# Row maxima of attention scores taken per head, with a signal for each, instead of per step of two heads

## The chip, the cores and the metric

The kernel runs on one core of a Trainium2 chip. The metric is the device time of one execution in microseconds (us). The engines are PE (TensorE: matmuls and, as PEld, their weight loads), DVE (VectorE), ACT (ScalarE), POOL (GpSimd) and SP (SyncE, which here only issues DMAs). Each engine works through its own list of instructions in order, and semaphores tie the lists together.

## The reference

Cross-attention over 64 samples. The input of each sample is normalised over all its 64 x 256 values, 8 heads of 64 channels attend from 256 queries to 256 keys of the context, and the result is projected and added to the input.

```python
# x: (64, 64, 256) = input (n, c, s); ctx_2048: (64, 64, 256) = context; h = 8 heads, c = 64 channels, all float32
mu = jnp.mean(input, axis=(1, 2), keepdims=True)
var = jnp.var(input, axis=(1, 2), keepdims=True)
xn = (input - mu) * jax.lax.rsqrt(var + EPS)
xn = xn * gamma[None, :, None] + beta[None, :, None]
q = jnp.einsum('oc,ncs->nos', Wq, xn) + bq[None, :, None]
kv = jnp.einsum('od,nds->nos', Wkv, context) + bkv[None, :, None]
q = q.reshape(n, h, c, s).transpose(0, 1, 3, 2)
kv = kv.reshape(n, 2 * h, c, -1).transpose(0, 1, 3, 2)
k, v = (kv[:, :h], kv[:, h:])
scale = c ** (-0.25)
att = jax.nn.softmax(jnp.einsum('nhqc,nhkc->nhqk', q * scale, k * scale), axis=-1)
y = jnp.einsum('nhqk,nhkc->nhqc', att, v)
y = y.transpose(0, 1, 3, 2).reshape(n, h * c, s)
out = jnp.einsum('co,nos->ncs', Wo, y) + bo[None, :, None]
return input + out
```

## The kernel before, in words

Two samples form a pair, and there are 32 pairs. A pair has 16 heads, which are worked on in eight steps of two heads each (`STEPS = 8`, `UNITS = 16`). The key and value projections are folded into other matrices at the start, so that the scores of a head are one product of transformed queries `t` with the raw context `c2`, and the attention result is a mix of context rows.

For step k of a pair these operations follow on each other:

1. `scores` (PE, L367): eight matmuls fill two banks of PSUM, `fill[k % 2][:, o, :]`, one bank of 512 columns for each head o (two query tiles of 256 keys). They wait until the exponentials of step k-2 have read both banks, and end with one signal, `scored`.
2. `row_max` (DVE, L538): one reduction reads both banks, 1024 columns, and writes the four negated maxima (2 heads x 2 query tiles). It ends with one signal, `max_ready`.
3. `exponentials` (ACT, L483): four activations of 256 columns, each followed by a read of its accumulator (the row sum). They wait for `max_ready` and signal `exp_ready` once per head.
4. `reciprocal` (DVE, L544): waits for both heads of the step.
5. `divide` (POOL, L639): 1024 columns, in place.
6. `turn` (DVE, L551): transposes the probabilities in blocks of 32, 1024 columns.
7. `mix` (PE, L401): items 0 to 3 belong to the pair's first sample, 4 to 7 to the second. Item 0 waits for transpose 3 (the transpose of step 3), and item 4 for transpose 7. The items 0 and 4 are followed by three more of their sample. After the items 3 and 7 ACT copies `z` (L499), and PE projects the output (L410).

Beside the steps run the normalisation of a pair ahead: statistics (DVE, L567), a matmul with ones for the mean (PE, L422), the small DVE operations of the spread (L577 to L583), a second such matmul (L426), the root (POOL, L649), the two normalisations (POOL, L654), the projection to `t` in `z` (PE, L379) and its copies (ACT, L492).

The order of the work on each engine is written out by hand. `PE_ORDER`, `ACT_ORDER`, `DVE_ORDER` and `POOL_ORDER` give each item a time in units of a sixteenth of a pair; each engine sorts its items by that time modulo 16, and an item whose time is 16 or more, or negative, belongs to the pair before, or to one ahead. Within one pair DVE runs, by this: transpose 5 of the pair before, max 0, reciprocal 7, the means, transpose 6, max 1, reciprocal 0, transpose 7 (still of the pair before), max 2, reciprocal 1, transpose 0, max 3, reciprocal 2, transpose 1, max 4, reciprocal 3, transpose 2, max 5, the spread, transpose 3, the result, reciprocal 4, the variance, max 6, the transpose of the context, reciprocal 5, max 7, transpose 4, the statistics, reciprocal 6. PE runs: scores 0 and 1, projection, scores 2, mixes 4 and 5 of the pair before, scores 3, mix 6, scores 4, mix 7, scores 5, the mean, the output projection, the spread's matmul, scores 6 and 7, mixes 0 to 3. ACT runs: copy of z, exponentials 0, the four copies to `t`, exponentials 1 to 3, copy of z, exponentials 4 to 7. POOL runs: divisions 0 to 3, division 4, root, division 5, the normalisations, divisions 6 and 7. A number behind an operation's name is always its step.

The DMAs are issued from SP, in an order of their own, and the change touches none of them.

Of the kernel before, what the change touches and what calls it, by code (L numbers as in the profile page):

```python
# [6 lines left out]
ALU = mybir.AluOpType  # L7
ACT = mybir.ActivationFunctionType
AX = mybir.AxisListType
# [12 lines left out]
UNITS = PS * H  # L22
STEPS = UNITS // 2
QT = S // 128
# [6 lines left out]
PAIRS_OF_BANKS = 2  # L31
# [60 lines left out]
def work(pair, order):  # L92
    for at, kind, item in in_order(order):
        owner = pair.shift(-int(at // UNITS))
        if owner.exists():
            yield kind, item, owner


def wait(eng, sem, value):
    if not isinstance(value, int) or value > 0:  # L100
        eng.wait_ge(sem, value)  # L101
# [6 lines left out]
def walk(eng, steps):  # L108
    for c in range(-3, 3):
        steps(Pair(0, c))  # L110
    with eng.Fori(0, (NPAIR - 8) // 2) as j:
        steps(Pair(j, 3))
        steps(Pair(j, 4))
    for c in range(NPAIR - 5, NPAIR + 2):
        steps(Pair(0, c))


def build(nc, x, ctx, gamma, beta, Wq, bq, Wkv, bkv, Wo, bo, out):
    stack = ExitStack()
    with stack:  # L120
        def sb(name, shape, dt=F32):
            return stack.enter_context(nc.sbuf_tensor(name, shape, dt))

        def pb(name, shape):
            return stack.enter_context(nc.psum_tensor(name, shape, F32))

        def sem(name):
            return stack.enter_context(nc.semaphore(name))
# [44 lines left out]
        t = [sb(f"t_{i}", [128, HP, PS, S]) for i in range(2)]  # L173
        neg_max = sb("neg_max", [128, STEPS, 2 * QT])
# [8 lines left out]
        fill = [pb(f"fill_{i}", [128, 2, 512]) for i in range(PAIRS_OF_BANKS)]  # L183
# [28 lines left out]
        max_ready = sem("max_ready")  # L212
# [19 lines left out]
        def load_weights(eng, weights, loaded):  # L232
            for dst, src in weights:
                eng.dma_start(dst, src, allow_slow_non_contiguous=True).then_inc(loaded, 16)  # L234
# [216 lines left out]
        @block.scalar  # L451
        def _(act):
            def query_key_steps():
                act.wait_ge(qk_loaded, 16 * QK_DMAS)
                act.mul(gamma_scaled[:, :], gamma2[:, :], SCALE).then_inc(w_act, 1)
                act.wait_ge(w_mm, 1)
                for i in range(2):
                    act.copy(qk[:, i::2, :], fill[0][:, i, 0:HP * CK].rearrange("r (p c) -> r p c", p=HP)
                             ).then_inc(w_act, 1)
                act.wait_ge(w_mm, 2)  # L460
                for i in range(2):
                    act.copy(wo_t2[:, :, i, :], fill[1][:, 1, 0:HP * C].rearrange("r (p c) -> r p c", p=HP)
                             ).then_inc(w_act, 1)
                act.wait_ge(w_dve, 3)

            def output_value_steps():
                act.wait_ge(w_mm, 4)
                banks = (fill[1][:, 1, :], fill[0][:, 1, :])
                for i in range(2):
                    r = 64 * i  # L470
                    act.copy(u[r:r + 64, :, :], banks[i][r:r + 64, 0:HP * C].rearrange("r (p c) -> r p c", p=HP)
                             ).then_inc(w_act, 1)

            def exponentials(pair, k):
                wait(act, max_ready, pair.count(STEPS, k + 1))
                owner, before = (pair, k - SLOTS) if k >= SLOTS else (pair.shift(-1), k - SLOTS + STEPS)
                if owner.exists():
                    wait(act, turned, owner.count(STEPS, before + 1))
                for o in range(2):
                    bank = fill[k % PAIRS_OF_BANKS][:, o, :]  # L480
                    for qt in range(QT):
                        g = QT * o + qt
                        ins = act.activation(probs[:, k % SLOTS, g, :], bank[:, K * qt:K * qt + K], ACT.Exp,  # L483
                                             bias=neg_max[:, k, g:g + 1], accum_out=denom[:, k, g:g + 1])
                    ins.then_inc(exp_ready, 1)

            def query_rows(pair, hp):
                if hp % 2 == 0:
                    wait(act, projected, pair.count(HP // 2, hp // 2 + 1))
                if pair.shift(-2).exists():  # L490
                    wait(act, scored, pair.shift(-2).count(STEPS, HP + hp + 1))
                act.activation(t[pair.parity()][:, hp, :, :], z[:, hp, :], ACT.Identity,  # L492
                               bias=d_col[:, hp:hp + 1]).then_inc(t_ready, 1)

            def copy_z(pair, s):
                wait(act, mixed, pair.count(PS, s + 1))
                if s == 0 and pair.shift(-1).exists():
                    wait(act, summed_out, pair.shift(-1).count(1, 1))
                act.copy(z_sb[:, s, :, :].rearrange("p h (t a j) -> p a (h t) j", t=QT, a=QB),  # L499
                         z[:, :, S * s:S * s + S].rearrange("p a (g j) -> p a g j", j=32)).then_inc(z_ready, 1)  # L500

            def steps(pair):
                for kind, item, owner in work(pair, ACT_ORDER):
                    if kind == "t":
                        if owner.first():
                            if item == 0:
                                query_key_steps()
                            elif item == 2:
                                output_value_steps()
                        query_rows(owner, item)  # L510
                    elif kind == "exp":
                        exponentials(owner, item)
                    else:
                        copy_z(owner, item)

            load_weights(act, qk_weights, qk_loaded)
            load_weights(act, out_weights, weights_loaded)
            walk(act, steps)

        @block.vector  # L520
        def _(dve):
# [13 lines left out]

            def row_max(pair, k):
                wait(dve, scored, pair.count(STEPS, k + 1))
                dve.tensor_reduce(neg_max[:, k, :],  # L538
                                  fill[k % PAIRS_OF_BANKS][:, :, :].rearrange("p o (t k) -> p (o t) k", t=QT),
                                  AX.X, ALU.max, negate=True).then_inc(max_ready, 1)  # L540

            def reciprocal(pair, k):
                wait(dve, exp_ready, pair.count(UNITS, 2 * k + 2))
# [53 lines left out]
            def steps(pair):  # L597
                for kind, item, owner in work(pair, DVE_ORDER):
                    if kind == "weights":
                        if owner.first() and item == 0:  # L600
                            query_key_steps()
                        elif owner.first():
                            output_value_steps()
                    elif kind == "max":
                        row_max(owner, item)
                    elif kind == "recip":
                        reciprocal(owner, item)
                    elif kind == "turn":
                        turn(owner, item)
                    elif kind == "moments":  # L610
                        channel_moments(owner)

                        wait(dve, moments_ready, owner.count(PS, PS))
                    elif kind == "mean_var":
                        channel_mean_var(owner)
                    elif kind == "spread":
                        channel_spread(owner)
                    elif kind == "sample_var":
                        sample_variance(owner)
                    elif kind == "turn_context":  # L620
                        turn_context(owner)
                    elif kind == "result":
                        result(owner)
# [66 lines left out]
```

## Time and profile before

| | us |
|---|---|
| median of 3 runs | 808.37 |
| lowest and highest of them | 806.89, 810.76 |
| the profiled execution | 807.66 |
| its span | 805.8 |
| mean granted TensorE clock | 0.983 of full |

The profile is of one execution. Its span goes from the first to the last instruction on the core; the execution's time is 1.86 us longer. The page gives the busy time of each engine and its share of the span. The timeline lists instructions with their start and their duration; a merged row has a count behind it (x8), and its duration reaches from the start of the first to the end of the last. In brackets stands the idle time of the engine ahead of the row and what ended it. On one engine an instruction may start before the recorded end of the one ahead of it.

### The profile page before, as it was taken

The page shows a single profiled execution, that of the slowest core. Times are in us where ns is not written, and L with a number is a line of the kernel's source. Part 1 is how long each engine was busy: PE and PEld are TensorE (multiplying, and loading weights), DVE is VectorE, ACT ScalarE, POOL GpSimd, SP SyncE. Part 2 cuts the span into 40 slices and gives each one's busy share as a digit, 9 for nine tenths or more (in the row PEclk, how much of TensorE's full clock was granted, in tenths as well). Part 3 has the DMA queues.
Part 4 walks back from the last instruction along what each step waited for, and adds up shares of the span by engine and source line. Part 5 has one row for each costly group of instructions (what it writes and reads, how often), then busy time and mean ns, then how long its engine had stood idle before and what let it go on. Part 6 is the DMA issues. An engine that isn't in the chain of part 4 may idle for free.

```text
span 805.8 us, 29956 instructions
## 1 busy us (share of the span) xinstructions
PE 686.3 (85%) x11204; PEld 445.8 (55%) x11204; DVE 678.0 (84%) x1124; ACT 621.6 (77%) x2248; POOL 581.7 (72%) x360
## 2 busy tenths in 40 slices
PE   5689988889888888988888988888898888898886
PEld 4355655555655555655555655555565555566453
DVE  1589888898988889898889898888989888989883
ACT  2578778787788878687878788878778778878872
POOL 1478677777777878677877777788777687777763
PEclk9989999999999999999999999999999999999998
DMA  5112222222221222222222221221222122222110
GB/s 111 37 48 68 62 57 67 60 62 62 62 63 51 72 52 64 59 62 53 68 59 58 62 64 52 64 72 51 62 62 62 49 72 53 64 65 52 44 40 15
DMA packets 74814, 47.56 MB, mean 59 GB/s; under 512 B 33748, under 2 KB 74708, under 8 KB 74772
## 3 DMA queue, kind: packets, MB, share of 16 engines
q1 hardware_dynamic: 72848, 46.59, 21.6%
q10 hardware_dynamic: 1924, 0.40, 0.3%
q8 instruction: 28, 0.46, 0.2%
q14 instruction: 14, 0.11, 0.0%
HBM read 25.96 MB, written 4.19 MB: 37 GB/s over the span
## 4 chain that ended last, share of the span: by engine, by line
POOL 41%; issue 37%; PE 9%; DVE 9%; ACT 2%; POOLq 1%; DMA 1%; SPq 1%; ACTq 0%; DVEq 0%
POOL probs L639 32%; POOL xhat L654 6%; DVE probs_t L551 4%; PE z L401 4%; DVE neg_max L538 3%; PE fill L367 3%; POOL rstd L649 3%; ACT probs L483 2%; POOLq L101 1%; PE z L379 1%; DMA wv<-in_L_xattn_Wkv 1%; ACT t L492 1%; DVE recip L544 0%; DVE y L594 0%; SPq L234 0%
## 5 line engine op out<-in xcount | busy, mean ns | idle before, releaser
L639 POOL TENSOR_TENSOR probs<-probs,recip 128x1024 f32<-128x1024 f32 x256 | 483.1, 1893 | 188.5 <-DVE recip L544 184.3
L483 ACT ACTIVATE probs<-fill,neg_max 128x256 f32<-128x256 f32 x1024 | 470.5, 483 | 149.9 <-DVE neg_max L538 149.6
L551 DVE STREAM_TRANSPOSE probs_t<-probs 128x1024 f32<-128x1024 f32 x256 | 313.7, 1225 | 49.7 <-POOL probs L639 46.2
L538 DVE TENSOR_REDUCE neg_max<-fill 128x4 f32<-128x1024 f32 x256 | 306.6, 1198 | 36.3 <-PE fill L367 36.0
L401 PE MATMUL z<-probs_t,ctx_keys 32*64 32x256 f32 x8192 | 260.3, 388 | 69.5 <-DVE probs_t L551 68.3
L367 PE MATMUL fill<-c,t 64*128 64x256 f32 x2048 | 285.6, 404 | 17.6 <-ACT probs L483 13.2
L401 PEld LDWEIGHTS z<-probs_t,ctx_keys 32*64 32x64 f32 x8192 | 177.0, 134 | 139.5 <-issue 69.7
L367 PEld LDWEIGHTS fill<-c,t 64*128 64x128 f32 x2048 | 182.8, 189 | 120.0 <-ACT probs L483 58.4
L483 ACT ACTIVATION_READ_ACCUMULATOR probs<-fill,neg_max 128x1 f32 x1024 | 220.1, 215 | 0.0
L492 ACT ACTIVATE t<-z,d_col 128x512 f32<-128x512 f32 x128 | 77.8, 708 | 7.3 <-PE z L379 7.3
L379 PE MATMUL z<-xhat,qk_gamma 64*128 64x512 f32 x256 | 66.5, 637 | 16.2 <-POOL xhat L654 16.2
L654 POOL TENSOR_SCALAR xhat<-x,mean,rstd 128x256 f32<-128x256 f32 x64 | 77.6, 1222 | 0.2
L499 ACT COPY z_sb<-z 128x1024 f32<-128x1024 f32 x64 | 65.4, 1021 | 11.5 <-PE z L401 10.5
L410 PE MATMUL z<-z_sb,u 128*64 128x256 f32 x512 | 62.3, 385 | 1.2 <-ACT z_sb L499 1.2
L379 PEld LDWEIGHTS z<-xhat,qk_gamma 64*128 64x128 f32 x256 | 23.1, 193 | 43.3 <-issue 38.3
L544 DVE RECIPROCAL recip<-denom 128x4 f32<-128x4 f32 x256 | 41.0, 160 | 6.3 <-ACT probs L483 2.7
L410 PEld LDWEIGHTS z<-z_sb,u 128*64 128x64 f32 x512 | 33.9, 136 | 16.6 <-ACT z_sb L499 2.3
L649 POOL TENSOR_TENSOR rstd<-variance,minus_half 128x2 f32<-128x2 f32 x32 | 22.8, 712 | 21.1 <-DVE variance L587 21.1
L567 DVE BATCH_NORM_STATS2 moments<-x 128x6 f32<-128x256 f32 x64 | 22.8, 398 | 9.3 <-DMA x<-in_x 9.3
L594 DVE SCALAR_TENSOR_TENSOR y<-z,out_bias,x_res 128x256 f32<-128x256 f32 x32 | 14.2, 445 | 9.6 <-PE z L410 9.6
L422 PEld LDWEIGHTS z<-mean_var,ones 128*128 128x128 f32 x64 | 10.1, 199 | 20.5 <-issue 16.5
L422 PE MATMUL z<-mean_var,ones 128*128 128x2 f32 x64 | 12.6, 267 | 8.1 <-DVE mean_var L571 6.7
(38 smaller groups left out, 91.1 us busy)
## 6 DMA issues: line engine op xcount, KB each, us to landing
ctx_keys<-ctx_turned SPq DMA_DIRECT2D x512, 32.0 KB, 1.8
x<-in_x SPq DMA_DIRECT2D x64, 128.0 KB, 2.8
c<-in_ctx SPq DMA_DIRECT2D x64, 128.0 KB, 2.7
ctx_rows<-in_ctx SPq DMA_DIRECT2D x128, 32.0 KB, 1.8
x_res<-in_x SPq DMA_DIRECT2D x32, 128.0 KB, 2.2
out<-y SPq DMA_DIRECT2D x32, 128.0 KB, 1.8
wq<-in_L_xattn_Wq ACTq DMA_DIRECT2D x2, 128.0 KB
wv<-in_L_xattn_Wkv SPq DMA_DIRECT2D x2, 128.0 KB
```

What stands on the lines that cost most here:

```text
L367: mm = pe.matmul(banks[:, o, K * qt:K * qt + K], t[p][r:r + 64, hp, s, 128 * qt:128 * qt + 128], c2[p][r:r + 64, s, :], start=True, stop=True)
L379: mm = pe.matmul(z[:, hp, :], qk_gamma[r:r + 64, 2 * hp:2 * hp + 2, :], xhat[r:r + 64, :, :], start=True, stop=True)
L401: mm = pe.matmul(z[64 * g:64 * g + 64, a, S * s:S * s + S], ctx_keys[p][r:r + 32, b, s, :], probs_t[p][r:r + 32, s, b, g, :, :, :], start= ...
L410: mm = pe.matmul(z[64 * s:64 * s + 64, 0, 0:S], u[:, hp, :], z_sb[:, s, hp, :], start=(hp == 0), stop=(hp == HP - 1))
L483: ins = act.activation(probs[:, k % SLOTS, g, :], bank[:, K * qt:K * qt + K], ACT.Exp, bias=neg_max[:, k, g:g + 1], accum_out=denom[:, k, ...
L492: act.activation(t[pair.parity()][:, hp, :, :], z[:, hp, :], ACT.Identity, bias=d_col[:, hp:hp + 1]).then_inc(t_ready, 1)
L499: act.copy(z_sb[:, s, :, :].rearrange("p h (t a j) -> p a (h t) j", t=QT, a=QB), z[:, :, S * s:S * s + S].rearrange("p a (g j) -> p a g j" ...
L538: dve.tensor_reduce(neg_max[:, k, :], fill[k % PAIRS_OF_BANKS][:, :, :].rearrange("p o (t k) -> p (o t) k", t=QT), AX.X, ALU.max, negate=T ...
L551: dve.transpose(probs_t[p][:, s, :, :, hp, :, :].rearrange("p b o t j -> p o t b j"), probs[:, k % SLOTS, :, :].rearrange("p (o t) (b j) - ...
L639: pool.tensor_tensor(p, p, recip[:, k, :].unsqueeze(2).broadcast_to([128, 2 * QT, K]), ALU.mult).then_inc(probs_ready, 1)
L649: pool.tensor_tensor(rstd[:, :], variance[:, :], minus_half[:, :], ALU.pow).then_inc(rstd_ready, 1)
L654: pool.tensor_scalar(xhat[:, s, :], x2[p][:, s, :], mean[:, s:s + 1], rstd[:, s:s + 1], ALU.subtract, ALU.mult).then_inc(xhat_ready, 1)
```

## The change

The maximum of a step is taken in two reductions, one for each head: 512 columns of one bank each, the first two and the last two of the step's four maxima. Each of them raises `max_ready`, which so counts heads (`UNITS`, 16 a pair) and no longer steps. ACT no longer waits ahead of the step's four activations for the step's maximum, but ahead of each head's two activations for the maximum of that head. The wait for `turned` (a free slot of `probs`) now stands ahead of the wait for the maximum. Nothing else is changed.

```diff
--- before.py
+++ after.py
@@ -472,11 +472,11 @@
                              ).then_inc(w_act, 1)
 
             def exponentials(pair, k):
-                wait(act, max_ready, pair.count(STEPS, k + 1))
                 owner, before = (pair, k - SLOTS) if k >= SLOTS else (pair.shift(-1), k - SLOTS + STEPS)
                 if owner.exists():
                     wait(act, turned, owner.count(STEPS, before + 1))
                 for o in range(2):
+                    wait(act, max_ready, pair.count(UNITS, 2 * k + o + 1))
                     bank = fill[k % PAIRS_OF_BANKS][:, o, :]
                     for qt in range(QT):
                         g = QT * o + qt
@@ -535,9 +535,10 @@
 
             def row_max(pair, k):
                 wait(dve, scored, pair.count(STEPS, k + 1))
-                dve.tensor_reduce(neg_max[:, k, :],
-                                  fill[k % PAIRS_OF_BANKS][:, :, :].rearrange("p o (t k) -> p (o t) k", t=QT),
-                                  AX.X, ALU.max, negate=True).then_inc(max_ready, 1)
+                for o in range(2):
+                    dve.tensor_reduce(neg_max[:, k, QT * o:QT * o + QT],
+                                      fill[k % PAIRS_OF_BANKS][:, o, :].rearrange("p (t k) -> p t k", t=QT),
+                                      AX.X, ALU.max, negate=True).then_inc(max_ready, 1)
 
             def reciprocal(pair, k):
                 wait(dve, exp_ready, pair.count(UNITS, 2 * k + 2))
```

## Rows read from the trace of the kernel before

**Rows 1.** The page, part 1: busy time of each engine.

```profile
PE 686.3 (85%) x11204; PEld 445.8 (55%) x11204; DVE 678.0 (84%) x1124; ACT 621.6 (77%) x2248; POOL 581.7 (72%) x360
```

**Rows 2.** Timeline of PE: start us, us, engine, line, operation, tiles, count.

```profile
66.11 0.36 PE L422 MATMUL z<-mean_var,ones 128*128 128x2 f32 x2
...
735.87 0.36 PE L422 MATMUL z<-mean_var,ones 128*128 128x2 f32 x2
```

**Rows 3.** Totals of the waits: engine, its line, releaser, us, times, longest.

```profile
ACT probs L483 <- DVE neg_max L538: 149.6, 118, 5.3
```

**Rows 4.** Timeline of DVE, first stretch of the pair; idle time in brackets.

```profile
421.31 1.23 DVE L538 TENSOR_REDUCE neg_max<-fill 128x4 f32<-128x1024 f32 x1 [0.91 <-PE fill L367]
...
426.00 1.19 DVE L538 TENSOR_REDUCE neg_max<-fill 128x4 f32<-128x1024 f32 x1
427.11 0.14 DVE L577 COPY mean<-z 128x2 f32<-128x2 f32 x1
...
429.15 0.17 DVE L544 RECIPROCAL recip<-denom 128x4 f32<-128x4 f32 x1
```

**Rows 5.** Timeline of POOL, the same pair.

```profile
429.39 1.89 POOL L639 TENSOR_TENSOR probs<-probs,recip 128x1024 f32<-128x1024 f32 x1 [2.48 <-DVE recip L544]
...
432.11 1.89 POOL L639 TENSOR_TENSOR probs<-probs,recip 128x1024 f32<-128x1024 f32 x1 [0.16 <-POOL rstd L649]
...
436.38 3.74 POOL L639 TENSOR_TENSOR probs<-probs,recip 128x1024 f32<-128x1024 f32 x2
```

**Rows 6.** Timeline of DVE, second stretch of the pair.

```profile
433.13 0.71 DVE L567 BATCH_NORM_STATS2 moments<-x 128x6 f32<-128x256 f32 x2
...
438.31 1.25 DVE L551 STREAM_TRANSPOSE probs_t<-probs 128x1024 f32<-128x1024 f32 x1 [1.28 <-POOL probs L639]
439.48 1.18 DVE L538 TENSOR_REDUCE neg_max<-fill 128x4 f32<-128x1024 f32 x1
...
440.67 1.21 DVE L551 STREAM_TRANSPOSE probs_t<-probs 128x1024 f32<-128x1024 f32 x1
...
445.10 1.22 DVE L538 TENSOR_REDUCE neg_max<-fill 128x4 f32<-128x1024 f32 x1 [0.73 <-PE fill L367]
```

**Rows 7.** Timeline of PE, the same pair.

```profile
423.31 1.12 PE L401 MATMUL z<-probs_t,ctx_keys 32*64 32x256 f32 x32
...
442.01 1.99 PE L401 MATMUL z<-probs_t,ctx_keys 32*64 32x256 f32 x64 [1.96 <-DVE probs_t L551]
443.92 1.14 PE L367 MATMUL fill<-c,t 64*128 64x256 f32 x8
```

**Rows 8.** Timeline of ACT, the same pair.

```profile
422.57 0.47 ACT L483 ACTIVATE probs<-fill,neg_max 128x256 f32<-128x256 f32 x1 [1.41 <-DVE neg_max L538]
...
424.54 1.01 ACT L499 COPY z_sb<-z 128x1024 f32<-128x1024 f32 x1
```

**Rows 9.** Groups by line and shape: count | busy us, mean ns | idle before.

```profile
L551 DVE STREAM_TRANSPOSE probs_t<-probs 128x1024 f32<-128x1024 f32 x256 | 313.7, 1225 | 49.7 <-POOL probs L639 46.2 <-issue 3.6
L538 DVE TENSOR_REDUCE neg_max<-fill 128x4 f32<-128x1024 f32 x256 | 306.6, 1198 | 36.3 <-PE fill L367 36.0
...
L567 DVE BATCH_NORM_STATS2 moments<-x 128x6 f32<-128x256 f32 x64 | 22.8, 398 | 9.3 <-DMA x<-in_x 9.3
...
L560 DVE STREAM_TRANSPOSE ctx_turned<-ctx_rows 128x256 f32<-128x256 f32 x32 | 13.9, 435 | 0.0
```

**Rows 10.** Timeline of all engines near the start of the run.

```profile
38.14 0.47 ACT L483 ACTIVATE probs<-fill,neg_max 128x256 f32<-128x256 f32 x1 [0.75 <-DVE neg_max L538]
...
40.13 2.08 PE L367 MATMUL fill<-c,t 64*128 64x256 f32 x8 [0.95 <-ACT probs L483]
...
42.25 1.23 DVE L538 TENSOR_REDUCE neg_max<-fill 128x4 f32<-128x1024 f32 x1 [0.60 <-PE fill L367]
```

**Rows 11.** Stretches: start:end, length, busy us (instructions) per engine, PEclk, DMA share, GB/s.

```profile
321.60:325.00 3.40, 3.30 (x66) 2.03 (x66) 2.29 (x3) 2.66 (x12) 2.70 (x2) 0.57 0.25 58
```

**Rows 12.** Timeline of PE, the mixes in that stretch.

```profile
321.70 3.35 PE L401 MATMUL z<-probs_t,ctx_keys 32*64 32x256 f32 x64 [2.42 <-DVE probs_t L551]
```

## The prediction

> **What bounds the kernel now.** I read the page's first part, then the totals of the waits, then the timeline of one steady pair on each engine, because the shares alone decide nothing here: PE is busy for 85%, DVE 84%, ACT 77%, POOL 72% [rows 1]. No engine is full, so the period of a pair (16 heads, eight steps) is set by a cycle that runs through several of them. It is regular: the matmul of the means, once per pair, starts at 66.11 us and 28 pairs on at 735.87, 23.92 us a pair [rows 2]; the pair that I walk takes 445.10 - 421.31 = 23.79 us from its max 3 (the maximum of step 3) to the next.
>
> ACT waits for the maxima for 149.6 us in 118 waits [rows 3], about 4.7 us in each of 32 pairs. That is what the change aims at. The question is whether this idle time lies on the cycle. I followed the cycle from max 3 at 421.31, which starts when its scores land:
> - DVE, with no idle time shown: max 3, reciprocal 2, transpose 1, max 4, reciprocal 3, transpose 2, max 5, the four small operations of the spread, transpose 3, the result, and reciprocal 4 at 429.15 [rows 4]. 7.84 us, three maxima in it.
> - Division 4 starts on POOL at 429.39, 0.24 us on. Behind it POOL runs root, division 5, the two normalisations, divisions 6 and 7, with no gap over 0.16 us [rows 5]. Division 6 ends at 436.38 + 1.89 = 438.27, and DVE's transpose 6, which waited for it, starts at 438.31 [rows 6]: 8.92 us, no maximum in it.
> - DVE: transpose 6, max 1, reciprocal 0, transpose 7, which ends at 440.67 + 1.21 = 441.88 [rows 6]; the mix that waits for it starts on PE at 442.01 [rows 7]. 3.70 us, one maximum.
> - PE: mixes 4 and 5, then scores 3 at 443.92 [rows 7], 1.91 us; and max 3 at 445.10 [rows 6], 1.18 us.
> The sum is 7.84 + 0.24 + 8.92 + 3.70 + 1.91 + 1.18 = 23.79 us, the period. No exponential is in it. Four maxima are: 1, 3, 4 and 5.
>
> **The change part by part.** *Removed:* the first head's exponentials wait no longer for the second head's half of the reduction. Now max 3 starts at 421.31 and the exponentials behind it at 422.57 [rows 4, 8], 1.26 us. How long a half takes: the same kind of operation stands in the trace at two sizes, the transpose with 1225 ns for 1024 columns and 435 ns for 256 [rows 9], so (1225 - 435) / 768 = 1.03 ns a column. 1024 columns are then 1055 ns, and the maximum's 1198 ns [rows 9] holds 143 ns that don't depend on columns. A half takes 527 + 143 = 670 ns, and the first exponentials can start 1198 - 670 = 0.53 us sooner.
>
> What that is worth in a steady pair: behind exponentials 3 ACT copies z at 424.54, and the copy also needs mix 7, which starts at 423.31 and takes 1.12 us, to 424.43 [rows 7, 8]. Of 0.53 us ACT can pass on 0.11 there. Mix 7 stands behind scores 3 in PE's order, so the cycle drives it. Exponentials 0 can start sooner, but the queries' rows behind them on ACT wait for the projection, which waits for POOL's normalisations in the cycle. Reciprocals 4 to 7 come late in DVE's own order and not when their exponentials end. So I value the earlier start at nothing; the POOL and DVE cycle is what covers it. Without that cover the gain is bounded by 0.53 us at one place of a pair.
>
> At the start of the run the cycle isn't closed yet: exponentials 3 wait 0.75 us for their maximum, scores 5 wait 0.95 us for these, and max 5 waits 0.60 us for the scores [rows 10]. The 0.53 us comes through once: -0.5 us. At the end the last z copies stand behind their mixes as above, so nothing there.
>
> *Added on DVE:* a second reduction per step, 256 in all, over the same columns. What it costs, d, decides the forecast. By the nearest rows: max 5 starts at 426.00 and the operation behind it at 427.11 [rows 4], so an overlapped maximum holds DVE for 1.11 us, 55 ns over its columns. The two statistics of 256 columns, like behind like, take 0.71 us together and 398 ns each [rows 6, 9]: the second starts 0.31 us behind the first, 48 ns over its 264 ns. From above: if the second half started only when the record of the first has ended, d would be the whole 143 ns. Zero and less is excluded, since the columns stay and one more instruction has to start. Between the ends I take the value of the rows in which one DVE operation follows another without waiting, 50 ns, and keep 40 to 143.
>
> The Trainium skill (Vector Engine (DVE) Microarchitecture Reference, Measured stream behaviour on trn2) gives built-in operations about 75 ns per instruction after queue overlap, beside the columns. The rows here show 48 and 55. By the page's figure the sum below would be 125 x 0.075 - 0.5 = +8.9 us, an estimate from that page.
>
> Where d counts: in the four maxima of the cycle, 4 x 50 = 0.20 us a pair. What is queued behind the longer maximum is the reciprocal and the transpose of older steps, and POOL's division and PE's mixes behind these; that is the cycle, counted once. Maxima 6, 7 and 0 lie between reciprocal 4 and the 1.28 us for which DVE waits before transpose 6, and max 2 lies ahead of the 0.73 us of wait before max 3 [rows 6]; 3d is 0.15 us, 0.43 at most, so these four are hidden. Without that cover d would count eight times, 0.40 us a pair.
>
> *Added on ACT:* one more wait per step. It is met when it is reached: the second half ends about 0.6 us behind the first, while the first head's two exponentials and their accumulator reads take 0.9 us of the step's 1.8. Its own handling can't be read from a row; between nothing and 0.1 us, 0.8 us a pair, it stays under the 4.7 us that ACT idles, so I take nothing. PE, SP and POOL get no instruction more and no DMA moves. The scores still wait for both heads' exponentials.
>
> *Sum:* 29 pairs x 4 maxima = 116, and about 9 more in the last two pairs, whose chain runs alike: 125 x 50 ns = +6.3 us, less 0.5 at the start, +5.8 us. The profiled execution took 807.66 us (span 805.8), which gives 813.5. The median of the three runs, 808.37, is 0.7 above it, so on the median 814.2 us, +0.7%.
>
> **The rivals.**
> A, faster: ACT's earlier start is passed on once in every pair. For it: 149.6 us is a large wait [rows 3], and POOL's spans are rough, so the cycle could be looser than it looks. Against it: six hops without an exponential add up to the period to 0.01 us. Its time: 0.53 - 0.20 = 0.33 us in 31 pairs, 10 us, 798. Its weak form passes on only the 0.11 us before the z copy, 3.4 us, with d small: 805. It decides from the point where the hop through ACT is longer than the one through POOL.
>
> B, no change: d is about 25 ns, or the 0.2 us a pair falls into a slack that I took for tight, as in the 0.24 us between reciprocal 4 and division 4. For it: tiny DVE operations follow each other closely. Its time: 125 x 0.025 - 0.5 = +2.6 us, 811. A difference under 0.5%, 4 us, is what a measurement of this kernel can hardly tell from none.
>
> C, slower by more: the halves don't overlap. Then 125 x 0.143 - 0.5 = +17.4 us, 826. Against it: 427.11 is 80 ns before the recorded end of max 5, 426.00 + 1.19 [rows 4]. The Trainium skill (VectorE: DVE Perf Modes, The DRAIN you can't avoid) says that the next operation starts only when the pipeline is empty. By the recorded ends the trace speaks against it for these operations.
>
> D, slower through the clock: in one pair mixes 4 and 5 take 3.35 us instead of 1.99, with a granted clock of 0.57 in that stretch (near 1.2 GHz, the lower level), after 2.42 us in which PE was idle [rows 11, 12]. They are on the cycle, so such a pair is 1.36 us longer. I found three such pairs in the run, one of them shown. The idle time before these mixes grows with d, and by up to the 0.53 us where exponentials 0 release scores 2 sooner. Six more such pairs are +8 us: 822. One or two fewer would take 1.4 us each off the forecast.
>
> That the exponentials don't start sooner at all I hold out: both sides count two signals a step, and each head has its own bank.
>
> **How the numbers follow.** The forecast's case (d from 40 to 80 ns, 812.9 to 817.9) 0.50; A 0.10; B 0.22; C 0.10; D 0.08. The range that leaves out no more than 2 in 10 goes from 806.5 (inside B with a clock drop or two fewer, and the edge of A) to 821. Slower by over 0.5%, above 812.4: nearly all of the forecast's case, C and D, 0.63. Within 0.5%: B, a rest of the forecast's, the weak form of A, 0.28. Faster by over 0.5%, below 804.3: 0.09.
>
> **What would show it.** Right: 512 reductions of some 670 ns, the second starting 0.58 us behind the first; the first exponentials starting 0.7 us behind their maximum's start; ACT's wait for maxima less by about 0.5 us a wait; 24.0 us a pair outside the clock drops; transpose 6 still waiting for POOL by about 1 us, and max 3 for its scores. Wrong: a pair of 23.7 us or less, or a division 4 that starts when exponentials end; then the cycle was another. More than five pairs with slow mixes would be D.

## The result and the profile after

The changed kernel takes 833.63 us in the median (831.77 to 837.62, four runs) beside 809.12 us for the kernel before on the same chip: a ratio of 1.031, 95% interval 1.027 to 1.036. It is slower by 25 us where 6 were forecast. The profiled execution took 837.62 us, with a span of 835.8; it is the slowest of the four, 4 us above their median. In all that follows the ratios leave out two stray executions, one of e4 with 994.69 us at a granted clock of 0.661 and one of e11 with 1698.96 us.

The page's first part and the groups of the maxima and of the mixes (columns as in [rows 1, 9]); behind them the wait that answers to [rows 3]:

```profile
span 835.8 us, 30356 instructions
PE 703.6 (84%) x11204; PEld 457.6 (55%) x11204; DVE 690.7 (83%) x1380; ACT 624.2 (75%) x2248; POOL 581.8 (70%) x360
L539 DVE TENSOR_REDUCE neg_max<-fill 128x2 f32<-128x512 f32 x512 | 322.7, 670 | 60.0 <-PE fill L367 59.8
L401 PE MATMUL z<-probs_t,ctx_keys 32*64 32x256 f32 x8192 | 276.5, 407 | 82.2 <-DVE probs_t L552 81.0
```

```profile
ACT probs L483 <- DVE neg_max L539: 150.3, 118, 4.8
```

A reduction of 512 columns takes 670 ns, as worked out. DVE is busy 12.7 us more, PE 17.3 us more with the same 11204 matmuls, and ACT's waits for maxima add up to as much as before.

The timeline of POOL, DVE and ACT in one undisturbed pair, which answers to [rows 4 to 8]:

```profile
301.62 3.75 POOL L640 TENSOR_TENSOR probs<-probs,recip 128x1024 f32<-128x1024 f32 x2
...
303.55 1.25 DVE L552 STREAM_TRANSPOSE probs_t<-probs 128x1024 f32<-128x1024 f32 x1 [1.13 <-POOL probs L640]
304.72 1.25 DVE L539 TENSOR_REDUCE neg_max<-fill 128x2 f32<-128x512 f32 x2
305.89 0.16 DVE L545 RECIPROCAL recip<-denom 128x4 f32<-128x4 f32 x1
...
310.41 1.29 DVE L539 TENSOR_REDUCE neg_max<-fill 128x2 f32<-128x512 f32 x2 [0.84 <-PE fill L367]
...
311.13 0.47 ACT L483 ACTIVATE probs<-fill,neg_max 128x256 f32<-128x256 f32 x1 [1.41 <-DVE neg_max L539]
```

The next instruction starts 305.89 - 304.72 = 1.17 us behind a step's first reduction, where it was 1.11 us: the second reduction costs d = 0.06 us. Two reductions together last 1.25 us and each of them 0.67, so the second starts 0.58 us behind the first. The exponentials start 311.13 - 310.41 = 0.72 us behind the start of their maximum instead of 1.26. Transpose 6 still waits for POOL, max 3 for its scores. All of that is what the forecast said. The means of the second pair start at 65.59 us instead of 66.11, 0.52 us sooner; that fits the forecast's -0.5 us at the start but doesn't show it, since with whole maxima they start between 65.48 (e7) and 66.44 us (e17) too.

The mixes 4 and 5 of successive pairs on PE, with the idle time before them, and the two means around an undisturbed pair and around a slow one:

```profile
155.65 3.42 PE L401 MATMUL z<-probs_t,ctx_keys 32*64 32x256 f32 x64 [2.52 <-DVE probs_t L552]
...
307.31 1.99 PE L401 MATMUL z<-probs_t,ctx_keys 32*64 32x256 f32 x64 [2.55 <-DVE probs_t L552]
314.77 0.38 PE L422 MATMUL z<-mean_var,ones 128*128 128x2 f32 x2 [0.18 <-ACT z_sb L499]
331.35 2.46 PE L401 MATMUL z<-probs_t,ctx_keys 32*64 32x256 f32 x64 [2.67 <-DVE probs_t L552]
333.75 2.08 PE L367 MATMUL fill<-c,t 64*128 64x256 f32 x8
340.31 0.38 PE L422 MATMUL z<-mean_var,ones 128*128 128x2 f32 x2
```

And the stretches of the first two of these mixes (columns as in [rows 11]):

```profile
155.60:159.20 3.60, 3.55 (x66) 2.23 (x68) 2.30 (x4) 2.41 (x11) 2.65 (x2) 0.58 0.22 52
307.30:309.30 2.00, 1.99 (x66) 1.47 (x66) 2.00 (x4) 1.91 (x9) 1.51 (x2) 1.00 0.21 49
```

The same 64 matmuls take 3.42 us at a granted clock of 0.58 (near the lower level, 1.2 GHz) and 1.99 us at 1.00 (2.4 GHz). The pair from 314.77 to 340.31 is 25.54 us long, with half-speed work in its mixes and in scores 3 behind them (2.08 us instead of 1.14).

To count, I take the start of the means of the second pair to that of the thirtieth, 28 pairs. Before: 25 undisturbed pairs of 23.77 us and three with a clock drop, of 25.17. After: ten undisturbed ones of 24.01 us and 18 with a clock drop, of 25.52. The 28 pairs took 669.8 us and now take 765.07 - 65.59 = 699.5, 29.7 us more. Of these 28 x 0.24 = 6.7 us are the longer pair, and 18 x 1.51 - 3 x 1.40 = 23.0 us are clock drops. The sum is the whole 29.7. An execution of the median length, 4 us shorter, would by an estimate have two or three slow pairs fewer.

### The profile page after: what moved, and what is told of

Its sections match the earlier page's. It is cut to its first block, busy times and chain, and to the rows that moved or that the text cites. A ratio compares the mean times of both kernels' runs of the same rounds, so it can differ in the third digit from the quotient of the medians.

```text
span 835.8 us, 30356 instructions
## 1 busy us (share of the span) xinstructions
PE 703.6 (84%) x11204; PEld 457.6 (55%) x11204; DVE 690.7 (83%) x1380; ACT 624.2 (75%) x2248; POOL 581.8 (70%) x360
## 4 chain that ended last, share of the span: by engine, by line
POOL 40%; issue 37%; DVE 9%; PE 9%; ACT 2%; POOLq 1%; DMA 1%; SPq 1%; DVEq 0%; ACTq 0%
POOL probs L640 31%; POOL xhat L655 6%; DVE neg_max L539 4%; PE z L401 4%; DVE probs_t L552 4%; PE fill L367 3%; POOL rstd L650 3%; ACT probs L483 2%; POOLq L101 1%; DMA wv<-in_L_xattn_Wkv 1%; ACT t L492 1%; PE z L379 0%; DVE y L595 0%; DVE recip L545 0%; SPq L234 0%
## 5 line engine op out<-in xcount | busy, mean ns | idle before, releaser
L483 ACT ACTIVATE probs<-fill,neg_max 128x256 f32<-128x256 f32 x1024 | 470.6, 483 | 151.5 <-DVE neg_max L539 150.3
L539 DVE TENSOR_REDUCE neg_max<-fill 128x2 f32<-128x512 f32 x512 | 322.7, 670 | 60.0 <-PE fill L367 59.8
L401 PE MATMUL z<-probs_t,ctx_keys 32*64 32x256 f32 x8192 | 276.5, 407 | 82.2 <-DVE probs_t L552 81.0
L367 PE MATMUL fill<-c,t 64*128 64x256 f32 x2048 | 290.3, 412 | 7.0 <-ACT probs L483 7.0
L401 PEld LDWEIGHTS z<-probs_t,ctx_keys 32*64 32x64 f32 x8192 | 183.1, 141 | 160.5 <-issue 107.5
L367 PEld LDWEIGHTS fill<-c,t 64*128 64x128 f32 x2048 | 188.9, 194 | 104.1 <-ACT probs L483 49.5
L499 ACT COPY z_sb<-z 128x1024 f32<-128x1024 f32 x64 | 64.8, 1012 | 37.9 <-PE z L401 37.4
```

Of the source, the lines that this page charges most:

```text
L367: mm = pe.matmul(banks[:, o, K * qt:K * qt + K], t[p][r:r + 64, hp, s, 128 * qt:128 * qt + 128], c2[p][r:r + 64, s, :], start=True, stop=True)
L401: mm = pe.matmul(z[64 * g:64 * g + 64, a, S * s:S * s + S], ctx_keys[p][r:r + 32, b, s, :], probs_t[p][r:r + 32, s, b, g, :, :, :], start= ...
L539: dve.tensor_reduce(neg_max[:, k, QT * o:QT * o + QT], fill[k % PAIRS_OF_BANKS][:, o, :].rearrange("p (t k) -> p t k", t=QT), AX.X, ALU.ma ...
```

## The experiments

All counts are of the profiled execution's same 28 pairs; "undisturbed" is the mean length of the pairs without slow mixes, and a slow pair is one with them. Ratios are to the kernel before on the same chip, with 95% intervals.

| run | us | ratio | undisturbed pair | slow pairs |
|---|---|---|---|---|
| before | 809 | 1 | 23.77 | 3 |
| changed | 833.6 | 1.027 to 1.036 | 24.01 | 18 |
| e1 split, ACT waits for both | 835.8 | 1.032 to 1.038 | 24.02 | 12 |
| e2 only step 0 split | 807.3 | 0.997 to 1.001 | 23.77 | 4 |
| e3 all but step 0 split | 836.6 | 1.031 to 1.038 | 24.00 | 16 |
| e4 changed, 4 added matmuls | 808.0 | 0.998 to 1.001 | 23.96 | 0 |
| e5 before, 4 added matmuls | 807.2 | 0.998 to 1.001 | 23.85 | 0 |
| e6 reciprocal 4 earlier | 808.2 | 0.999 to 1.002 | 23.38 | 10 |
| e15 one small operation | 808.8 | 0.998 to 1.002 | 23.83 | 1 |
| e7 three | 823.3 | 1.014 to 1.021 | 23.94 | 9 |
| e16 five | 843.0 | 1.032 to 1.048 | 24.05 | 23 |
| e8 eight | 835.6 | 1.023 to 1.036 | 24.24 | 9 |
| e9 steps 0, 2, 6, 7 split | 806.9 | 0.997 to 1.000 | 23.77 | 2 |
| e10 e6 + 3 added matmuls | 807.5 | 0.997 to 0.999 | 23.56 | 6 |
| e11 e10, reciprocal 4 earlier still | 815.7 | 1.005 to 1.010 | 23.61 | 6 |
| e12 e11 with maxima per head | 803.9 | 0.991 to 0.996 | 23.25 | 9 |
| e14 e6 + 5 matmuls, early | 791.2 | 0.976 to 0.982 | 23.36 | 0 |
| e13 e12 + 6 matmuls, early | 778.8 | 0.961 to 0.966 | 23.01 | 0 |
| e17 e13 with whole maxima | 781.5 | 0.964 to 0.968 | 23.03 | 0 |
| e18 changed + 6 matmuls, early | 809.5 | 0.999 to 1.002 | 24.02 | 0 |

**Which half of the change: the second reduction or the earlier signal.** My first theory was that exponentials 0, ending sooner, let scores 2 run sooner, so that PE idles longer before the mixes. e1 takes the earlier signal away:

```diff
+                wait(act, max_ready, pair.count(UNITS, 2 * k + 2))
                 for o in range(2):
-                    wait(act, max_ready, pair.count(UNITS, 2 * k + o + 1))
```

> Two reductions per step on DVE as in the changed kernel, but ACT waits for both of them before the step's first exponential, so nothing is released sooner. Theory 1 (the exponentials of step 0 end sooner, scores 2 run sooner, PE then idles longer before mixes 4 and 5 and the clock falls in that idle time): the idle time before the mixes stays near 2.4 and 2.0 us, at most five pairs have slow mixes, pairs take about 24.0 us, and the time is about 815 us (before + 125 x 0.06 us less nothing at the start). Theory 2 (the longer DVE work alone makes the clock fall): 15 or more pairs with slow mixes and about 833 us.

e2 and e3 split chosen steps only, by a list `SPLIT` of `(0,)` and `(1, ..., 7)`:

```diff
+                if k not in SPLIT:
+                    dve.tensor_reduce(neg_max[:, k, :], ...).then_inc(max_ready, 1)
+                    return
```

> Only step 0 has its maximum taken in two reductions with a signal each; the other seven steps are as before. Theory 1: the reduction of step 0 is not on the cycle, so an undisturbed pair stays at 23.8 us, but scores 2 run sooner in every second pair, the idle time before mixes 4 and 5 is 2.5 us or more in every pair, and 12 to 20 pairs have slow mixes at 1.4 to 1.5 us each: 822 to 830 us. Theory 2: the cycle is not longer, so the clock falls no more often than before, 807 to 810 us.

> The mirror of the run with step 0 alone: steps 1 to 7 take two reductions with a signal each, step 0 one. Theory 1: idle time before mixes 4 and 5 about 2.5 and 2.0 us, at most five pairs with slow mixes, 24.0 us a pair and 814 us. Theory 2: as slow as the changed kernel, about 833 us.

The mixes in e1, then in e2:

```profile
298.60 1.99 PE L401 MATMUL z<-probs_t,ctx_keys 32*64 32x256 f32 x64 [1.96 <-DVE probs_t L552]
322.65 2.54 PE L401 MATMUL z<-probs_t,ctx_keys 32*64 32x256 f32 x64 [2.39 <-DVE probs_t L552]
```

```profile
322.88 1.99 PE L407 MATMUL z<-probs_t,ctx_keys 32*64 32x256 f32 x64 [2.61 <-DVE probs_t L564]
346.67 1.99 PE L407 MATMUL z<-probs_t,ctx_keys 32*64 32x256 f32 x64 [2.57 <-DVE probs_t L564]
```

The first theory falls, twice. e1 has the idle time of before (1.96 and 2.39 us against 1.96 and 2.42) and is as slow as the changed kernel. e2 has the long idle time in every pair (2.6 us) and is as fast as before. The earlier signal does no harm; what is left is the second reductions, in steps other than step 0.

**The two reductions, or the length of the pair.** e7, e8, e15 and e16 keep whole maxima and put three, eight, one or five copies of one column on DVE behind reciprocal 2, on the cycle and away from the idle time before the mixes:

```diff
                 dve.reciprocal(recip[:, k, :], denom[:, k, :]).then_inc(recip_ready, 1)
+                if k == 2:
+                    for i in range(3):
+                        dve.tensor_copy(spare[:, i:i + 1], ones[:, i:i + 1])
```

> The kernel before, every maximum in one reduction, with three copies of one column (SBUF to SBUF, 0.07 us each) on DVE behind reciprocal 2, which lies on the cycle but not in the hop that ends PE's idle time before mixes 4 and 5. That idle time stays at 2.4 and 2.0 us; a pair takes 24.0 us as in the changed kernel. Theory 3 (the number of clock drops follows from the length of a pair, 24.0 instead of 23.8 us): 12 to 20 slow pairs, 825 to 837 us. Theory 4 (the drops come from the two reductions themselves): at most five slow pairs, 813 to 815 us.

> The same with eight such copies: 24.3 to 24.4 us a pair. Theory 3a (the longer the pair, the more slow pairs): 20 or more of them, 850 us or more. Theory 3b (only some lengths of a pair meet the clock's fall again and again): fewer slow pairs than at 24.0 us, at most 8, 825 to 837 us. Theory 4: at most five, 825 us.

> The kernel before with one copy of a column behind reciprocal 2: 23.85 us a pair. Theory 3 (the length of a pair decides): between the counts at 23.8 and 24.0 us, 3 to 9 slow pairs, 809 to 819 us. Theory 4 (the reductions): 3, 809 to 811 us.

> With five such copies: 24.1 us a pair. Theory 3: 9 to 16 slow pairs, 828 to 838 us. If the two reductions themselves add slow pairs at the same length of a pair, no more than 9, 828 us or less.

The copies in e8, eight of them in 388.36 - 387.89 = 0.47 us, 0.06 us each:

```profile
387.89 0.55 DVE L548 COPY spare<-ones 128x1 f32<-128x1 f32 x8
388.36 1.24 DVE L555 STREAM_TRANSPOSE probs_t<-probs 128x1024 f32<-128x1024 f32 x1
```

The mixes of two pairs of e16:

```profile
285.17 2.49 PE L402 MATMUL z<-probs_t,ctx_keys 32*64 32x256 f32 x64 [2.46 <-DVE probs_t L555]
294.13 0.38 PE L423 MATMUL z<-mean_var,ones 128*128 128x2 f32 x2
310.72 3.48 PE L402 MATMUL z<-probs_t,ctx_keys 32*64 32x256 f32 x64 [2.01 <-DVE probs_t L555]
319.67 0.38 PE L423 MATMUL z<-mean_var,ones 128*128 128x2 f32 x2
```

No maximum is split there, the idle times are those of before within 0.05 us, and the clock falls more often than in the changed kernel. So split maxima aren't needed, and the count of slow pairs comes with the length of the pair. It doesn't grow steadily with it: 10 at 23.38 us, 3 at 23.77, 1 at 23.83, 9 at 23.94, 12 to 23 at 24.00 to 24.05, 9 at 24.24. e8 fits theory 3b in its time, with nine slow pairs where at most eight were expected, and with more of its cost in the pairs themselves (28 x 0.47 = 13 us) and less in drops. The other three missed their ranges: e7 (nine slow pairs, 823.3 us) and e15 (one, 808.8 us) stayed below them, e16 (23, 843.0 us) went above. The direction was theory 3's, but the length of the pair doesn't give the count.

**Only the maxima on the cycle.** e9 splits the four steps that the walk puts beside the cycle, with `SPLIT = (0, 2, 6, 7)`.

> Two reductions with a signal each in steps 0, 2, 6 and 7, the four steps whose maxima the prediction puts beside the cycle; steps 1, 3, 4 and 5 keep one. If only the maxima of the cycle set the length of a pair, and the length of a pair sets the number of clock drops: 23.8 us a pair, three to five slow pairs, 807 to 810 us. If every second reduction counts alike: 23.9 to 24.0 us a pair, nine or more slow pairs, 822 us or more.

Its pairs have the length of before to 0.01 us and two of them are slow, though 256 reductions of 512 columns run in it. Its time, 806.9 us, is that of before. This confirms which four maxima count.

**The cycle itself.** e6 moves one item of DVE's order:

```diff
-             + at('recip', 3.87, 6.23, 7.93, 9.58, 12.65, 13.80, 15.96, 17.68)
+             + at('recip', 3.87, 6.23, 7.93, 9.58, 12.30, 13.80, 15.96, 17.68)
```

> The kernel before with one item of DVE's order moved: reciprocal 4 ahead of the result. If the cycle of the prediction is right, its hop to division 4 gets shorter by the result's 0.36 us and a pair takes 23.4 to 23.5 us: 796 to 799 us unless the clock falls more often at this period; if the rate of clock drops depends on the length of a pair, it may be anything from 0 to 20 slow pairs, which the mix durations show. If the cycle is wrong (the exponentials set the period), nothing changes: 807 to 810.

The result's place on DVE before is 429.15 - 428.78 = 0.37 us long, with reciprocal 4 at 429.15 [rows 4]:

```profile
428.78 0.44 DVE L594 SCALAR_TENSOR_TENSOR y<-z,out_bias,x_res 128x256 f32<-128x256 f32 x1
```

The undisturbed pair is 0.39 us shorter. The cycle is the right one, and 28 pairs x 0.39 = 11 us are gained; ten slow pairs instead of three give them back, so the time stands still. Nearly every third pair is slow, in regular order. In the changed kernel it is two of every three from the eleventh counted pair on, and in e1, after ten undisturbed ones, likewise.

**PE's idle time as the condition.** e4 and e5 put matmuls whose result is used by nothing in front of mix 4:

```diff
-                    wait(pe, turned, pair.count(STEPS, STEPS))
                     wait(pe, z_ready, pair.count(PS, 1))
                     if pair.shift(2).exists():
                         wait(pe, t_ready, pair.shift(2).count(HP, HP))
+                    for _ in range(4):
+                        pe.matmul(z[:, 0, S * s:S * s + 128], ones[:, :], ones[:, :], start=True, stop=True)
+                    wait(pe, turned, pair.count(STEPS, STEPS))
```

> The changed kernel with four matmuls added on PE in front of mix 4 (ones by ones, 128 columns each, into a part of z that mix 4 then overwrites; their result is used by nothing). They start when the queries' rows of the pair ahead have been copied, so PE idles about 1.2 us and not 2.6 before it has work. Both theories have the slow clock come from PE's idle time there: no or few pairs with slow mixes, 24.0 us a pair, 810 to 813 us. If the slow mixes come from something else (another engine's activity, the chip), they stay: about 833 us, and more if the added matmuls delay mix 4.

> The kernel before with the same four matmuls in front of mix 4. If PE's idle time there is what lets the clock fall, its three slow pairs go too: 807.7 - 3 x 1.4 = 803.5 us in a profile, about 804.5 in the median, 23.8 us a pair, and the distance to the changed kernel with the same matmuls is the pure cost of the second reductions, 125 x 0.06 less 0.5 at the start = 4 to 7 us less than the changed one's 808.0 (so 801 to 804). If only the changed kernel's drops hang on it: no change to before, 808 to 809.

PE in e4, two pairs:

```profile
415.88 1.16 PE L397 MATMUL z<-ones 128*128 128x128 f32 x8 [0.86 <-ACT t L494]
417.62 1.99 PE L403 MATMUL z<-probs_t,ctx_keys 32*64 32x256 f32 x64 [0.58 <-DVE probs_t L554]
...
440.28 1.16 PE L397 MATMUL z<-ones 128*128 128x128 f32 x8 [1.18 <-ACT t L494]
441.58 1.99 PE L403 MATMUL z<-probs_t,ctx_keys 32*64 32x256 f32 x64
```

No slow pair is left in either, and the changed kernel is back at the time of before (0.998 to 1.001) with its reductions as they are, 2 us below its range. e5 missed its range: its drops are gone, but every second pair got longer behind the added matmuls (23.65 and 24.14 us in turn, 23.85 in the mean), so the two kernels came out 0.1% apart, not 0.6. e18 adds six matmuls that start when only the first query copy is done and don't delay mix 4:

> The changed kernel in its own order with the six matmuls that leave PE no long idle time before mixes 4 and 5. No slow pair; 24.0 us a pair, because four second reductions of 0.06 us lie on the cycle: 807 to 810 us, that is 7 us over what before would take without its three slow pairs (803.5).

24.02 us a pair and 809.5 us, as expected: the second reductions cost the 7 us of the forecast over 28 pairs. Before loses 3 x 1.40 = 4.2 of them in its own drops, which leaves 737.59 - 65.15 = 672.4 us against 669.8. The profiled executions as a whole are only 0.4 us apart; the rest lies outside the counted pairs, before the first and behind the last.

**Versions that are faster.** e10 to e14 and e17 join the earlier reciprocal with added matmuls. e11 moves it ahead of transpose 3 too (11.50 in the list); e13, e14, e17 and e18 start six or five matmuls early:

```diff
+                        wait(pe, t_ready, pair.shift(2).count(HP, 1))
+                    for _ in range(6):
+                        pe.matmul(z[:, 0, S * s:S * s + 128], ones[:, :], ones[:, :], start=True, stop=True)
+                    if pair.shift(2).exists():
```

> Reciprocal 4 ahead of the result in the kernel before, and three of the added matmuls in front of mix 4. Without the clock drops its pairs of 23.4 us should show: 31 x 0.40 = 12 us and its own ten drops less, 795 to 797 us, with no slow pair. If the drops stay, 808 us.

> The same with reciprocal 4 ahead of transpose 3 too: the hop from max 3 to division 4 is shorter by 1.16 us more. If the cycle through POOL stays the longest, 22.3 us a pair and 761 us; DVE is then busy for 21.5 us of a pair, and the exponentials, the scores and the mixes of the first sample come near the cycle, so a pair of 22.5 to 23.0 us and 765 to 783 us is the likelier result.

> The same on the changed kernel: maxima per head, reciprocal 4 ahead of transpose 3, three matmuls in front of mix 4. If with the shorter hop the wait for a step's maximum lies on the longest chain, the earlier signal is worth more than the second reduction costs, and it is faster than the run with whole maxima by up to 0.3 us a pair, 10 us. If POOL and DVE still set the pair, it is slower by 0.2 to 0.5 us a pair, 6 to 15 us.

> The run with maxima per head, reciprocal 4 ahead of transpose 3 and added matmuls, but six matmuls that start when the first of the four query copies is done, so that PE has under 0.3 us of idle between scores 2 and mix 4. If that idle time brought its nine slow pairs, they go: 803.9 - 9 x 1.5 = 790 to 793 us, 23.3 us a pair. If not: 802 to 806.

> Whole maxima, reciprocal 4 ahead of the result, five added matmuls that start at the same early point. If the idle time brought the slow pairs: none left, 23.4 to 23.6 us a pair, 796 to 801 us. If not: 806 to 809.

> The fastest run so far (778.8 us, maxima per head, reciprocal 4 ahead of transpose 3, six added matmuls) with whole maxima again. If the exponentials' wait for a maximum lies on the longest chain once the hop to division 4 is short, this is slower, by 0.2 to 0.4 us a pair: 785 to 792 us, 23.2 to 23.5 us a pair. If POOL and DVE still set the pair, it is faster by about 0.2 us a pair: 772 to 776 us.

e10 and e11 missed: their pairs were only 0.2 us shorter than before's and six of them slow. Why the pairs didn't get shorter shows in e11 on ACT, DVE and PE:

```profile
415.31 0.47 ACT L485 ACTIVATE probs<-fill,neg_max 128x256 f32<-128x256 f32 x1 [1.19 <-DVE neg_max L540]
...
417.12 2.44 ACT L494 ACTIVATE t<-z,d_col 128x512 f32<-128x512 f32 x4
...
418.48 1.21 DVE L553 STREAM_TRANSPOSE probs_t<-probs 128x1024 f32<-128x1024 f32 x1
...
419.61 0.94 PE L397 MATMUL z<-ones 128*128 128x128 f32 x6 [1.18 <-ACT t L494]
...
420.47 1.98 PE L403 MATMUL z<-probs_t,ctx_keys 32*64 32x256 f32 x64
```

Transpose 7 ends at 419.69, but the mixes start only at 420.47, behind the added matmuls, and these wait for ACT's query copies, which stand behind exponentials 0 and their maximum. The added matmuls made a second path, through ACT. PE in e10 shows a slow pair:

```profile
488.95 1.65 PE L397 MATMUL z<-ones 128*128 128x128 f32 x6 [1.18 <-ACT t L494]
490.53 2.79 PE L403 MATMUL z<-probs_t,ctx_keys 32*64 32x256 f32 x64
```

There the clock is already down in the added matmuls, behind 1.18 us of idle (1.65 us for what takes 0.94 at full speed). With that stretch filled too, e14 and e13 have no slow pair, and both were faster than expected, by 5 and 11 us. PE in e13, the means being one pair apart:

```profile
434.02 0.38 PE L426 MATMUL z<-mean_var,ones 128*128 128x2 f32 x2 [0.18 <-ACT z_sb L503]
...
446.51 1.13 PE L367 MATMUL fill<-c,t 64*128 64x256 f32 x8 [0.48 <-ACT probs L487]
447.57 1.60 PE L397 MATMUL z<-ones 128*128 128x128 f32 x12
449.58 1.99 PE L405 MATMUL z<-probs_t,ctx_keys 32*64 32x256 f32 x64 [0.40 <-DVE probs_t L556]
...
456.97 0.38 PE L426 MATMUL z<-mean_var,ones 128*128 128x2 f32 x2
```

e13 beats both kernels: 778.8 us, 0.963 of before. Maxima per head don't make it so: with whole maxima (e17) it is 781.5 us, the intervals 0.961 to 0.966 and 0.964 to 0.968 overlap, and the undisturbed pairs are 23.01 and 23.03 us. That is between the two ranges expected of e17. e12 against e11 was 803.9 against 815.7 us, a gain for maxima per head with a shorter pair (23.25 against 23.61), even with nine slow pairs against six. That is rival A's mechanism, on the path of the rows above: exponentials 0 wait 1.19 us for their maximum there, and the mixes hang on them. With the matmuls begun early the earlier signal is no longer worth anything that can be told.

## Why the prediction was wrong

**The cycle: right.** Six hops without an exponential. e6 shortened one by 0.37 us and the pair by 0.39; e9 put reductions beside it, and nothing moved.

**The earlier exponentials are worth nothing in a steady pair: right.** They start 0.54 us sooner behind their maximum, and e1, without the earlier signal, has the same undisturbed pair (24.02 and 24.01 us). But ACT's wait for maxima did not shrink by 0.5 us a wait: it is 150.3 us in 118 waits, as against 149.6. ACT's waits in e1, then its waits for mixes ahead of the copy of z, in before, after and e1:

```profile
ACT probs L483 <- DVE neg_max L539: 170.6, 118, 5.4
```

```profile
ACT z_sb L499 <- PE z L401: 10.5, 4, 9.3
ACT z_sb L499 <- PE z L401: 37.4, 61, 8.1
ACT z_sb L499 <- PE z L401: 10.2, 3, 9.6
```

With both reductions but no earlier signal the wait is 170.6 us, so the signal takes away some 20 us, 0.17 us a wait. ACT idles about as much elsewhere instead: it now waits for the mixes ahead of its copies of z, 37.4 us in all and not 10.5. That is the place at which the prediction let ACT pass on only 0.11 of its 0.53 us.

**The cost of the second reduction: right, 0.06 us where I took 0.05,** and 4 x 0.06 = 0.24 us a pair, measured 0.24. The Trainium skill (Vector Engine (DVE) Microarchitecture Reference, Measured stream behaviour on trn2) has about 75 ns per instruction, somewhat above this trace's 60. The recorded fixed part, 143 ns, would be the price of halves that don't overlap at all, rival C; this trace has not half of it. The Trainium skill (VectorE: DVE Perf Modes, The DRAIN you can't avoid) lets the next operation wait until the pipeline is empty and adds that one which isn't held starts earlier; these reductions behave as the addition says, with a next operation 80 ns ahead of the recorded end.

**The sum: the term left out is the clock.** The failed step is the one in rival D and in the sum, "Six more such pairs are +8 us", at a chance of 0.08, with the forecast's sum holding the three drops unchanged. It was 15 more pairs at 1.5 us each, 23.0 us of 29.7 in the profiled execution. That slow mixes are on the cycle, what one costs and where it happens was right. Its cause as I gave it, an idle time before the mixes that grows, was wrong: e1 and e2 show it from both sides. What the runs put in its place is the length of the pair: 0.2 us more of it, from second reductions or from small copies (e7, e16), takes the slow pairs from three to nine and more; with PE's idle time filled (e18) there are none and the forecast's +7 us is all that is left of the change. The prediction gives no reason for holding the count at three. In the trace of before the three slow mixes stand behind 2.24, 2.42 and 1.96 us of idle time and undisturbed ones behind the same values, the 1.96 us in [rows 7] for one: the idle time doesn't tell them apart.

**Left open.** What in the chip makes one pair length meet the fall again and again and another not, and why the count is low at 23.8 and high at 23.4 and 24.05, no run shows. Nor do they give a limit on the idle time: e10 has 1.18 us before its added matmuls and six slow pairs, e4 has up to the same 1.18 us there and none, and e18 none with up to 1.23 us before its mixes; the length of the pair and the number of added matmuls differ. That it is the filled idle time and not the added work as such that keeps the clock up is argued from where the clock falls; no run put the same matmuls elsewhere in the pair. The counts are of one profiled execution each, and others differ: the times go from 830.8 to 842.1 us in e1 and from 836.0 to 848.3 in e16, some seven or eight drops apart. So the runs tell few drops at 23.8 us from many at 24.0, but don't put e1, e3, e16 and the changed kernel in order, or e8 safely below them.

## What to carry to other kernels

Write down the cycle that sets the period before pricing an edit: here it priced the change and e6 to 0.04 us per pair and showed that a wait of 150 us was worth nothing. It holds only while that cycle is the longest: in e11 another, through ACT, took over, and the 22.3 us of the cycle alone became 23.6. But where the trace shows even a few repetitions with TensorE at the lower clock behind an idle time that all repetitions have, price the case in which all of them get it, here 31 x 1.5 = 46 us: a change of the period by 1 to 2% can bring a good part of it, in either direction. Here matmuls without use in the idle time took the slow pairs away in e4, e5, e13, e14, e17 and e18, though not in e10 to e12, and only with the slow pairs gone did shorter hops bring more than 1%.

## What the runs showed of the hardware

- Falls of the clock, counted in one profiled execution each, came with the length of a regular period, and not in step with it: 3 of 28 at 23.77 us, 23 of 28 at 24.05, 9 at 24.24, 10 at 23.38. In before and the changed kernel a slow pair costs 1.4 to 1.5 us, though the slow stretch may begin in the middle of the mixes.
- Five copies of one column (0.06 us each on DVE) made a kernel of 808 us slower by 3.2 to 4.8%. Over the 28 pairs of the profiled execution that is 707.9 - 669.8 = 38 us, 28 x 0.28 = 8 us by longer pairs and 30 by slow ones.
- Two reductions back to back cost 0.06 us more than one of twice the columns, at 670 ns recorded for each half and 1198 for the whole.
